# Cross-attention decoder layer: queries and keys staged by two heads, values fetched behind them, and some low parts moved to the vector engine

## The reference

```python
# 1: gated feed-forward; of each token's 2752 gate values the smaller half (by magnitude) is set to 0
s = silu(x @ w_gate.T)
_, idx = top_k(-abs(s), 1376);  s[rows, idx] = 0
x = layernorm(x + (s * (x @ w_up.T)) @ w_down.T)
# 2: attention over the context: 32 query heads of 32, 8 key/value heads, 4 query heads share one of those
q = x @ Wq;  k = ctx @ Wk;  v = ctx @ Wv
out = softmax(q k^T / sqrt(32)) v
x = layernorm(x + out @ Wo)
# 3: linear layer with 4-bit weights, in bfloat16
x = layernorm(x + (x.bf16 @ dequantize(qweight, qscale, qzeros).bf16.T))
```

## Time and profile before

| | |
|---|---|
| runs | 2545.92, 2547.3, 2553.11 us; median 2547.3 us |
| profiled execution | 2557.08 us, with a span of 2555.3 us from the first to the last instruction |
| PE busy | 95% of the span |
| POOL, DVE, ACT busy | 55%, 49%, 41% |
| DMA | 371.70 MB, mean 145 GB/s |
| mean granted TensorE clock | 0.972 of 2.4 GHz |

### The profile page before, as it was taken

The page is one execution under the profiler, slowest core; times in us unless marked ns, Lnnn a source line. Parts: engine busy times, 40 slices in busy tenths (PEclk is TensorE's granted clock), DMA queues, the critical chain, the costliest instruction groups (busy, mean ns, idle before and its releaser), DMA issues. The chain is left out here.

```text
span 2555.3 us, 32587 instructions
## 1 busy us (share of the span) xinstructions
PE 2423.3 (95%) x12640; PEld 2106.2 (82%) x12640; DVE 1264.0 (49%) x1775; ACT 1045.8 (41%) x1531; POOL 1414.6 (55%) x630
## 2 busy tenths in 40 slices
PE   7999899999999999999999999999988888888998
PEld 6999899988999889999889998899966565565775
DVE  3772303961017830069400485345467776664665
ACT  2112234533337333364323553233267676672211
POOL 5343244865447755458554585454378787783221
PEclk9999899999999999999999999999989898898999
DMA  5555522333333333233333233689957675556773
GB/s 195 175 194 169 205 94 92 107 120 126 117 101 103 122 118 119 99 100 123 111 118 116 96 108 100 192 252 291 256 159 176 161 170 142 140 139 164 178 174 98
DMA packets 245995, 371.70 MB, mean 145 GB/s; under 512 B 124336, under 2 KB 176560, under 8 KB 245584
## 3 DMA queue, kind: packets, MB, share of 16 engines
q1 hardware_dynamic: 245840, 369.60, 48.7%
HBM read 290.15 MB, written 78.70 MB: 144 GB/s over the span
## 5 line engine op out<-in xcount | busy, mean ns | idle before, releaser
L968 POOL TENSOR_TENSOR gp_w_lo<-cy_raw,gp_w_hi 128x1024 fp32r<-128x1024 f32 (+2 forms) x300 | 724.5, 2416 | 614.2 <-ACT gp_w_hi L847 613.7
L180 PE MATMUL gp_acc<-gp_x_hi,gp_w_hi 128*128 128x448 f32 x1504 | 561.0, 373 | 11.1 <-DVE gp_x_lo L1065 8.6
L181 PE MATMUL gp_acc<-gp_x_lo,gp_w_hi 128*128 128x448 f32 x1504 | 552.1, 367 | 0.0
L182 PE MATMUL gp_acc<-gp_x_hi,gp_w_lo 128*128 128x448 f32 x1504 | 551.9, 367 | 0.0
L847 ACT CAST gp_w_hi<-cy_raw 128x1024 fp32r<-128x1024 f32 (+2 forms) x300 | 307.1, 1026 | 308.6 <-PE gp_acc L182 307.1
L1413 POOL TENSOR_TENSOR ap_e_lo<-ap_e,ap_e_hi 125x1344 fp32r<-125x1344 f32 x112 | 341.7, 3072 | 99.4 <-DVE ap_e_hi L1494 69.0
L180 PEld LDWEIGHTS gp_acc<-gp_x_hi,gp_w_hi 128*128 128x128 f32 x1504 | 284.2, 189 | 35.8 <-issue 7.4
L182 PEld LDWEIGHTS gp_acc<-gp_x_hi,gp_w_lo 128*128 128x128 f32 x1504 | 284.2, 189 | 22.4
L181 PEld LDWEIGHTS gp_acc<-gp_x_lo,gp_w_hi 128*128 128x128 f32 x1504 | 284.6, 189 | 21.0
L464 DVE TENSOR_REDUCE gp_sel_unit<-gp_keys 112x4 f32<-112x2048 f32 x4 | 9.1, 2286 | 549.5 <-ACT gp_keys L860 549.5
L180 PE MATMUL gp_acc<-gp_h_hi,gp_w_hi 128*128 128x448 f32 (+1 forms) x704 | 267.3, 380 | 8.4 <-DVE gp_h_lo L1030 5.6
(11 more groups left out here) (192 smaller groups left out, 4350.4 us busy)
## 6 DMA issues: line engine op xcount, KB each, us to landing
cy_raw<-in_w_gu SPq DMA_DIRECT2D x172, 512.0 KB, 3.2
cy_raw<-in_w_d SPq DMA_DIRECT2D x80, 512.0 KB, 3.5
cp_c_raw<-in_ctx_t SPq DMA_DIRECT2D x32, 750.0 KB, 6.5
cy_raw<-in_w_q SPq DMA_DIRECT2D x32, 512.0 KB, 4.1
...
```

The lines of the kernel that those rows point to most:

```text
L180: nc.tensor.matmul(out, wh, xh, start=first, stop=False)
L181: nc.tensor.matmul(out, wh, xl, start=False, stop=False)
L182: return nc.tensor.matmul(out, wl, xh, start=False, stop=last)
L968: last = nc.gpsimd.tensor_tensor(o, i, hi.bitcast(F32), ALU.subtract)
```

## The change

Queries and keys are laid out in DRAM and in SBUF by two key heads (`NQK = 4` quarters) and fetched by quarters, each with its own semaphore and its own condition; all indices `h // 4` and `h % 4` become `h // 2` and `h % 2`. Each row of a fetch is half as long. The store of keys in the context stage becomes two DMAs of 64 rows.

In the attention stage SP's order is new: quarter 3 of batch n + 1 at h = 0, quarters 0, 1 and 2 of batch n + 2 at h = 2, 4 and 6 (after steps 6, 12 and 18 of batch n), the load of Wo at h = 3, the values at h = 5, and the inverted sums at h = 7 with DVE's reciprocal at step 22.

At the start of the gated stage all four parts of x are already loaded, the last two into the places of raw tiles 2 and 3; those two tiles are loaded once DVE has read x. DVE makes the low part of the first weight tile. In batch 15 DVE makes the low parts of heads 2, 5 and 7, and its quotients stand at steps 14 and 17.

The diff, cut to what the prediction speaks of (semaphore counts of 64 for 48, and plain changes of index, are left out):

```diff
@@ -29,6 +29,7 @@
 KN = C // KT
+NQK = 4
 VW = 2 * HD + 2
...
@@ -87,17 +89,17 @@
         self.qs, self.ks = [None, None], [None, None]
-        self.qs[0] = m.sb("qs0", [3 * HD + 2, 2, REP, 4, S], F32R)
-        self.ks[0] = m.sb("ks0", [3 * HD + 2, 2, 4, CP], F32R)
+        self.qs[0] = m.sb("qs0", [3 * HD + 2, NQK, REP, 2, S], F32R)
+        self.ks[0] = m.sb("ks0", [3 * HD + 2, NQK, 2, CP], F32R)
         self.vs0 = m.sb("vs0", [KN, KT, KV, VW], F32R)
         m.jump(self.QK1)
-        self.qs[1] = m.sb("qs1", [3 * HD + 2, 2, REP, 4, S], F32R)
-        self.ks[1] = m.sb("ks1", [3 * HD + 2, 2, 4, CP], F32R)
+        self.qs[1] = m.sb("qs1", [3 * HD + 2, NQK, REP, 2, S], F32R)
+        self.ks[1] = m.sb("ks1", [3 * HD + 2, NQK, 2, CP], F32R)
         m.jump(self.DEN)
...
         m.jump(self.SMALL)
-        self.n_max = m.sb("n_max", [S, 2, REP, 4], F32)
+        self.n_max = m.sb("n_max", [S, NQK, REP, 2], F32)
         self.nm_hi = m.sb("nm_hi", [H, S], F32R)
...
@@ -107,12 +109,14 @@
         self.o_hi, self.o_lo = m.sb("o_hi", [P, KV, P], F32R), m.sb("o_lo", [P, KV, P], F32R)
+        self.x_more = [self.raw[2 + i][:, 0:2 * T].rearrange("p (k t) -> p k t", t=T) for i in range(2)]
+        self.more_loaded = [m.sem(f"more_loaded{i}") for i in range(2)]
         self.x_loaded = [m.sem(f"x_loaded{i}") for i in range(self.XR)]
...
         self.q_stored = [m.sem(f"q_stored{i}") for i in range(self.NQO)]
-        self.qk_loaded = [[m.sem(f"qk_loaded{i}{h}") for h in range(2)] for i in range(2)]
+        self.qk_loaded = [[m.sem(f"qk_loaded{i}{f}") for f in range(NQK)] for i in range(2)]
         self.v_loaded = [m.sem(f"v_loaded{i}") for i in range(2)]
...
@@ -123,21 +127,22 @@
         for s in self.c_stored:
-            eng.wait_ge(s, 48 * (B // 2))
+            eng.wait_ge(s, 64 * (B // 2))
         eng.wait_ge(self.w3_stored, 16)
...
-    def fetch_qk(self, sp, qd, kd, n, half):
+    def fetch_qk(self, sp, qd, kd, n, f):
         p, stack = n % 2, 3 * HD
-        q_rows = self.qs[p][:, half].bitcast(F32).rearrange("d j m q -> d (j m q)")
-        k_rows = self.ks[p][:, half].bitcast(F32).rearrange("d v c -> d (v c)")
-        for dst, src in ((q_rows[0:2 * HD], qd[n, half]), (k_rows[0:HD], kd[n, half, 0:HD]),
-                         (q_rows[2 * HD:stack], qd[n, half, 0:HD]), (k_rows[HD:stack], kd[n, half])):
-            sp.dma_start(dst, src).then_inc(self.qk_loaded[p][half], 16)
+        q_rows = self.qs[p][:, f].bitcast(F32).rearrange("d j m q -> d (j m q)")
+        k_rows = self.ks[p][:, f].bitcast(F32).rearrange("d v c -> d (v c)")
+        key = kd[n, 2 * (f % 2) + f // 2]
+        for dst, src in ((q_rows[0:2 * HD], qd[n, f]), (k_rows[0:HD], key[0:HD]),
+                         (q_rows[2 * HD:stack], qd[n, f, 0:HD]), (k_rows[HD:stack], key)):
+            sp.dma_start(dst, src).then_inc(self.qk_loaded[p][f], 16)
...
@@ -241,7 +246,9 @@
                 sp.wait_ge(evac, NB * n + 2)
-                sp.dma_start(kd[n].rearrange("m s d v c -> (d v) m s c"), k_out[p][:].bitcast(F32)).then_inc(stored[p], 16)
+                for w in range(2):
+                    sp.dma_start(kd[n, 2 * w:2 * w + 2].rearrange("m s d v c -> (d v) m s c"),
+                                 k_out[p][2 * HD * w:2 * HD * (w + 1)].bitcast(F32)).then_inc(stored[p], 16)
                 sp.wait_ge(evac, NB * n + NB)
...
@@ -264,10 +271,11 @@
                 if n == B - 3:
-                    for i in range(cy.RAW):
+                    for i in range(2):
                         sp.dma_start(cy.raw[i][:], w_gu[i]).then_inc(cy.raw_loaded[i], 16)
-                        if i < cy.XR:
-                            sp.dma_start(cy.x_raw[i][:], x_t[0, :, 2 * i:2 * i + 2]).then_inc(cy.x_loaded[i], 16)
+                        sp.dma_start(cy.x_raw[i][:], x_t[0, :, 2 * i:2 * i + 2]).then_inc(cy.x_loaded[i], 16)
+                    for i in range(2):
+                        sp.dma_start(cy.x_more[i], x_t[0, :, 4 + 2 * i:6 + 2 * i]).then_inc(cy.more_loaded[i], 16)
             sp.wait_ge(copied, KD)
...
@@ -742,6 +749,8 @@
                     sp.wait_ge(lo_done, n - RAW + 1)
+                else:
+                    sp.wait_ge(x_lo_done, n + 1)
                 if n >= N:
...
@@ -787,13 +796,11 @@
                 for s in range(2):
-                    sp.dma_start(qd[g, :, j // 4, s].rearrange("b d j m q -> (d j) m b q")[:, j % 4],
+                    sp.dma_start(qd[g, :, j // 2, s].rearrange("b d j m q -> (d j) m b q")[:, j % 2],
                                  q_out[q % NQO][:, s, :].bitcast(F32).rearrange("p (b q) -> p b q", q=S)
...
-            for i in range(XR, XC):
-                load_x(0, i)
-            for n in range(RAW, NALL + AHEAD + 4):
+            for n in range(XR, NALL + AHEAD + 4):
                 if n < NALL:
...
@@ -815,16 +822,19 @@
                         sp.wait_ge(s, 32 * KD // NQO)
-                    cy.fetch_qk(sp, q_v, k_v, 0, 0)
+                    for f in range(2):
+                        cy.fetch_qk(sp, q_v, k_v, 0, f)
                 if p == 23:
-                    cy.fetch_qk(sp, q_v, k_v, 0, 1)
+                    for f in range(2, NQK):
+                        cy.fetch_qk(sp, q_v, k_v, 0, f)
                 if p == 26:
...
                     sp.wait_ge(back, 2 * B)
-                    cy.fetch_qk(sp, q_v, k_v, 1, 0)
+                    for f in range(2):
+                        cy.fetch_qk(sp, q_v, k_v, 1, f)
                 if p == 32:
...
@@ -849,9 +859,8 @@
                 x = XC * g + i
-                act.wait_ge(x_loaded[x % XR], 16 * (x // XR + 1))
-                if g > 0:
-                    act.wait_ge(used, N_CH * (g - 1) + DOWN)
+                act.wait_ge(x_loaded[x % XR], 16 * (x // XR))
+                act.wait_ge(used, N_CH * (g - 1) + DOWN)
                 nc.scalar.copy(x_hi[:, XK * i:XK * i + XK, :], x_raw[x % XR][:]).then_inc(x_hi_done, 1)
...
@@ -910,10 +919,15 @@
-            for i in range(XC):
-                if i < SPL:
-                    split_hi(i)
-                x_split_hi(0, i)
+            split_hi(0)
+            for i in range(XR):
+                act.wait_ge(x_loaded[i], 16)
+                nc.scalar.copy(x_hi[:, XK * i:XK * i + XK, :], x_raw[i][:]).then_inc(x_hi_done, 1)
+            for i in range(XR, XC):
+                act.wait_ge(cy.more_loaded[i - XR], 16)
+                nc.scalar.copy(x_hi[:, XK * i:XK * i + XK, :], cy.x_more[i - XR]).then_inc(x_hi_done, 1)
+            for n in range(1, SPL):
+                split_hi(n)
             for g in range(G):
...
@@ -986,8 +1000,9 @@
             pool.wait_ge(pads, 1)
-            for i in range(SPL):
-                split_lo(i)
+            pool.wait_ge(lo_done, 1)
+            for n in range(1, SPL):
+                split_lo(n)
             for g in range(G):
...
@@ -1054,16 +1069,18 @@
                 dve.wait_ge(cy.scored, y + 1)
-                nc.vector.reduce_max(cy.n_max[:, hh // 4, 2 * a:2 * a + 2, hh % 4], p_s[y % 2][:, :, 0:C],
+                nc.vector.reduce_max(cy.n_max[:, hh // 2, 2 * a:2 * a + 2, hh % 2], p_s[y % 2][:, :, 0:C],
                                      AX_X).then_inc(cy.maxed, 1)
...
             sel.start()
+            dve.wait_ge(hi_done, 1)
+            nc.vector.tensor_tensor(w_lo[0][:], raw[0][:], w_hi[0][:].bitcast(F32), ALU.subtract).then_inc(lo_done, 1)
             for i in range(XC):
...
                 dve.wait_ge(x_hi_done, i + 1)
-                nc.vector.tensor_tensor(x_lo[:, k, :], x_raw[i % XR][:], x_hi[:, k, :].bitcast(F32),
-                                        ALU.subtract).then_inc(x_lo_done, 1)
+                nc.vector.tensor_tensor(x_lo[:, k, :], x_raw[i][:] if i < XR else cy.x_more[i - XR],
+                                        x_hi[:, k, :].bitcast(F32), ALU.subtract).then_inc(x_lo_done, 1)
             cy.await_context(dve)
...
@@ -1271,14 +1288,16 @@
     TURN_AT = 18
-    RECIP_AT = 20
-    QUOTIENTS_AT = (17, 20)
+    RECIP_AT = 22
+    QUOTIENTS_AT = (14, 17)
     FULL = (3,)
...
     NE, NHI, NLO, NO = 4, 3, 3, cy.NO
-    W_LOAD_AT, W_SPLIT_AT = 2, 6
+    W_LOAD_AT, W_SPLIT_AT = 3, 6
+    V_AT = 5
+    LO_LAST = (2, 5, 7)
...
@@ -1329,15 +1348,25 @@
+        def by_dve(g):
+            return g // KV == B - 1 and g % KV in LO_LAST
+
+        def lo_of_pool(g):
+
+            return upto(LO_POOL, g) - sum(by_dve(x) for x in range(g + 1))
+
         def await_lo(eng, g):
-            eng.wait_ge(lo_pool, upto(LO_POOL, g))
+            if by_dve(g):
+                eng.wait_ge(lo_dve, LO_LAST.index(g % KV) + 1)
+            else:
+                eng.wait_ge(lo_pool, lo_of_pool(g))
...
         def _(sp):
-            def fetch_qk(n, half):
+            def fetch_qk(n, f):
                 if n >= 2:
-                    sp.wait_ge(t_scored, NX * (n - 2) + NX // 2 * (half + 1))
-                cy.fetch_qk(sp, qd, kd, n, half)
+                    sp.wait_ge(t_scored, NX * (n - 2) + NX // NQK * (f + 1))
```

(37 more changed lines are left out.)

29 lines of the change are left out of this document (14 added, 15 removed).

## The result

The changed kernel takes 2585.04 us (median of four runs, 2580.17 to 2586.4) against 2546.61 us before: ratio 1.0143, 95% interval 1.012 to 1.0167, so slower by about 38 us where 16 were forecast. The profiled executions differ by 29.1 us (spans 2584.4 and 2555.3). Timed again, the changed kernel takes 2582.42 us and the kernel before, in thirteen runs beside it, 2555.2: ratio 1.0115 (1.0088 to 1.0143), 27 us. So most of what lies between 38 and 27 us is the kernel before, whose first four runs were 8.6 us shorter than these thirteen.

The account below looks back on a forecast made before the run. The prediction saw TensorE 95% busy, stalled in attention by DMAs behind values on five engines. It summed +18.3 - 4.5 + 1.5 = +15.3 us, put on the 2547.3 median: 2563 us, range 2502 to 2590.

Parts of the forecast that it names:

- The keys' wait: Attention stage: PE waits 30.7 us in all for late keys; forecast to cost nothing with fetches by two heads.
- A: Start of the next batch's first scores (L1558) on PE; forecast at T + 10.2, ordinarily T + 7.9 to 8.1 before.
- T: The mark: PE's transposition of the maxima (L1549), once in each batch of the attention stage.
- rows not held: Rival: rows of maxima pass what stands on the five engines, landing at T + 5.6; 2498 us, chance 0.20.
- Values drain sooner: Rival, faster or even: values never slowed, rows of maxima land at T + 8.3; 2536 us, chance 0.12.
- Short rows cost: Rival: half-long rows have a fixed price, so values begin later, rows of maxima at T + 12; 2588 us, chance 0.10.
- the case that came true: Main forecast, held rows: maxima's rows wait behind values and quarter 2 on five engines; 2563 us, chance 0.58.
- part 3: Start of the gated stage: x already loaded, DVE makes the first weight's low part; -4.5 us (3.5 to 5.2).
- part 1: Attention stage, queries and keys fetched by two heads: 14 intervals 418.6 against 400.3 us, +18.3 (bounds -8.3 and +47.7).
- part 4: Closing batch: DVE makes three of seven low parts, quotients go ahead of head 5's cast; +1.5 us (-3 to +4).
- the sum for the landing: Rows of maxima: from T + 8.0, values 4.7 later, quarter instead of half -2.1, one output store fewer -0.4: T + 10.2.
- Part 2: Context stage, keys stored in two DMAs a batch, 16 issues of 0.4 us on a waiting SP: costs nothing.

Follow-up runs that it names:

- second pair of profiles: Both kernels, unchanged, profiled and timed again: the changed kernel 2582.4 us, ratio 1.0115, against the kernel before at 2555.2 us.
- one cut: Kernel before with each fetch of values cut in two parts, 112 and 13 rows: 2498.2 us, ratio 0.9775.
- the order set right: Changed kernel with values cut in two parts and the rows of maxima issued ahead of quarter 2: 2487.0 us, ratio 0.9732 to the kernel before.

## Why the prediction was right or wrong

**Direction and mechanism were right.** The slower side was the likeliest, and for the reason given: the rows of maxima stand behind the values, which run on five engines, and behind quarter 2's share of the same five. The keys' wait goes, A lies beyond T + 10, and no interval is at 33 us by a reciprocal. The share of 0.3 ahead of A lasts about one microsecond, not two. Taking away either of the two in front (values at head 3, or rows first) takes away all of the loss and more. The rival "rows not held" fell, even with a queue of their own. "Values drain sooner" fell too. "Short rows cost" gave nearly the measured time, 2588, but for a reason that no run bears out: halving the bytes of quarter 2 with as many rows moved A by 1.8 us, which is half of what the forecast charged for the bytes of the whole. No run has the same bytes in longer rows.

**The size was wrong.** The time lies in the stated range, 2502 to 2590, but above the 2545 to 2582 of the case that came true, and the move was more than twice the one forecast. Against the second pair of profiles, spans 2579.6 and 2552.8, the difference of 26.8 us has these parts:

| part | forecast | measured |
|---|---|---|
| up to the first mark (part 3) | -4.5 | -7.5 |
| 14 intervals (part 1) | +18.3 | +33.4 |
| behind the last mark (part 4) | +1.5 | +1.0 |

**The step that failed** is the sum for the landing, T + 8.0 + 4.7 - 2.1 - 0.4 = T + 10.2, mis-sized by 1.2 us: it measured T + 11.4 in thirteen batches, 15.6 us in all. The first batch was 2.3 us better than forecast (T + 7.9), since its values still went out early (at T - 5.2). The pace of PE behind it, 19.7 us, was right (19.8). In that sum quarter 2 had 3.7 us (1.6 for slowing the values, 2.1 behind them) and all the rest T + 6.5. Quarter 2 was not priced too low: with it issued behind the rows A is 2.6 us earlier, and with half of its bytes 1.8, which in proportion is 3.6 for the whole. So the short term is the rest, the values and the rows' own way: T + 7.8 to T + 8.8 in place of T + 6.5. My bounds, T + 8.3 to T + 12.3, held the value.

Which piece of that rest is short, no run separates. It is not the pace of the values alone, which is 133 to 139 GB/s in the changed kernel as in the earlier trace rows. One assumption in it is seen to fail: the values were to run alone from T - 1.0 to T + 2.0, but in all thirteen ordinary batches of the second profile the share jumps to 0.83 or more (0.83 to 0.98) in the half microsecond from T + 0.5, when only the output store of T - 0.8 can have come to them. The forecast let them be slowed by quarter 2 only. A slip in its working went the other way: counted back 4.2 us from 1969.9 the values of the kernel before end at T + 2.6, not T + 2.2, and with that the same sum gives about T + 9.8.

**The base** was the second error. Putting the sum on 2547.3 took three runs as exact; the 9.8 us between them and the profiled execution were a warning that the kernel's own time is spread by that much. On 2555.2 the same sum gives 2570.5, against 2582.4.

**Part 2** at nothing: the context stage ends no later than before. **Part 3**: the first tile starts 2.1 us earlier, and its 24 products take 7.5 us in place of 11.4; in the trace their spacing falls from 0.37 to 0.20 us at 313.6, so the clock rises inside the tile, which I had allowed for at the edge only. Part of the -7.5 us up to the first mark is the context stage's jitter (it ends 0.4 us earlier in this pair of profiles, 0.9 in the first). **Part 4** has PE's wait for head 5's cast as foreseen (6.4 us), and is worth +1.0 or less.

**What I missed** was the larger thing. I named the five engines as the cause of the keys' wait, worked out what they do to this change, and did not ask what their removal would give: 56 us on the kernel before by one cut, 95 us on the changed one with the order set right.
